# GpSimd makes the two bf16 parts of the negated row maxima, and its turn runs in another order

## What is computed

```
ada = silu(c) @ W_ada + b_ada                      # six modulation vectors
h = layernorm(x) * (1 + scale_msa) + shift_msa
q, k, v = split(h @ W_qkv + b_qkv)                 # 16 heads of 9 channels
attn = softmax(q * 9**-0.5 @ k.T)                  # over 256 tokens
x = x + gate_msa * (attn @ v @ W_proj + b_proj)
h = layernorm(x) * (1 + scale_mlp) + shift_mlp
x = x + gate_mlp * (gelu(h @ W_fc1 + b_fc1) @ W_fc2 + b_fc2)
U = qr(P).Q;  A = skew(silu(c) @ W.T + b);  R = expm(A)
out = x + ((x @ U) @ R - x @ U) @ U.T              # a rotation in 64 dimensions
```

## Time and profile before

| | us |
|---|---|
| three timed runs | 388.78, 390.67, 393.87 |
| their median | 390.67 |
| the profiled execution | 386.43 |
| its span, first to last instruction | 384.6 |

### The profile page before, as it was taken

One profiled execution on the slowest core, in us unless ns is written; L12 is line 12 of the kernel. 1 busy time (PEld: TensorE's weight loads), 2 busy tenths in 40 slices (PEclk: granted clock), 3 DMA queues, 4 the chain that ended last, 5 costly groups with the idle time before them and its releaser, 6 DMA issues.

```text
span 384.6 us, 7566 instructions
## 1 busy us (share of the span) xinstructions
PE 315.6 (82%) x2645; PEld 191.5 (50%) x2645; DVE 255.3 (66%) x791; ACT 144.6 (38%) x262; POOL 113.1 (29%) x271
## 2 busy tenths in 40 slices
PE   2888866986987889797889798989759999996687
PEld 1333423543444445454546455556546666664556
DVE  6856668578768877879888888864433554555433
ACT  2111113576674553545554555554202223321010
POOL 5813505006019046026053152020261333300000
PEclk9999998699998885899998998999957999999855
DMA  3922311114511212201212100000000000000003
GB/s 116 282 69 84 93 51 46 49 56 104 158 30 45 84 41 53 71 18 49 79 46 62 36 3 3 2 3 2 3 0 0 2 0 1 2 0 2 0 1 123
DMA packets 20202, 17.95 MB, mean 47 GB/s; under 512 B 3524, under 2 KB 18005, under 8 KB 20040
## 3 DMA queue, kind: packets, MB, share of 16 engines
q1 hardware_dynamic: 19556, 16.34, 15.6%
q10 hardware_dynamic: 610, 1.14, 1.0%
HBM read 12.28 MB, written 4.81 MB: 44 GB/s over the span
## 4 chain that ended last, share of the span: by engine, by line
PE 57%; DVE 27%; issue 7%; POOL 4%; ACT 3%; DMA 0%; DVEq 0%; POOLq 0%; ACTq 0%
DVE nm L912 11%; PE pst L264 10%; PE m L642 5%; PE m L483 5%; PE ps L449 5%; PE pst L265 5%; DVE gp L722 3%; PE m L286 3%; PE pst L470 3%; PE m L270 3%; PE pst L381 3%; DVE gm L723 2%; PE m L264 2%; PE pst L490 2%; DVE nmb L922 2%
## 5 line engine op out<-in xcount | busy, mean ns | idle before, releaser
L912 DVE TENSOR_REDUCE nm<-ps 128x2 f32<-128x512 f32 x128 | 87.7, 689 | 32.3 <-PE ps L449 29.2
L1144 ACT ACTIVATE pex<-pst 128x1024 f32<-128x1024 f32 x64 | 65.6, 1025 | 28.5 <-PE pst L470 27.8
L449 PE MATMUL ps<-ks,qs 54*128 54x256 bf16 x256 | 29.5, 309 | 29.3 <-DVE nm L912 28.7
L751 DVE TENSOR_SCALAR pm<-m 64x1 f32<-64x1 f32 x64 | 13.6, 213 | 43.7 <-PE m L286 43.2
L1434 POOL TENSOR_TENSOR qkr<-qk,parts 96x768 f32<-96x768 f32 x6 | 9.8, 1636 | 103.7 <-ACT parts L1125 103.7
L483 PE MATMUL m<-pex,ve 128*32 128x256 f32 x512 | 37.7, 416 | 0.0
L1447 POOL TENSOR_TENSOR xin<-xin,res 128x288 f32<-128x288 f32 x16 | 12.8, 799 | 76.3 <-DVE res L941 76.3
L449 PEld LDWEIGHTS ps<-ks,qs 54*128 54x128 bf16 x256 | 11.4, 102 | 42.5 <-issue 37.2
L270 PE MATMUL m<-gm,ident 64*64 64x65 f32 x126 | 24.3, 282 | 7.0 <-DVE gm L723 3.9
L286 PE MATMUL m<-qst,ident 64*64 64x64 f32 (+42 forms) x128 | 19.9, 235 | 11.1 <-DVE qst L757 11.1
L470 PE MATMUL pst<-qs,ks 56*128 56x256 bf16 x256 | 27.6, 295 | 1.0 <-ACT pex L1144 0.7
(11 more groups left out here) (246 smaller groups left out, 584.4 us busy)
## 6 DMA issues: line engine op xcount, KB each, us to landing
scr_qk<-parts SPq DMA_DIRECT2D x24, 144.0 KB, 2.0
qs<-scr_qk SPq DMA_DIRECT2D x96, 36.0 KB
ks<-scr_qk SPq DMA_DIRECT2D x72, 36.0 KB
gates<-scr_ada SPq DMA_DIRECT2D x2, 576.0 KB, 6.6
out_dram<-xin SPq DMA_DIRECT2D x8, 144.0 KB, 1.9
wr<-in_L_cond_W_dram SPq DMA_DIRECT2D x1, 1134.0 KB
xin<-in_x_dram SPq DMA_DIRECT2D x1, 864.0 KB, 5.4
ks<-scr_qk ACTq DMA_DIRECT2D x24, 36.0 KB
```

The source lines that it names most:

```text
L449: ins = mm(ps[e][:, L * i:L * i + L], qs[64 * e:64 * e + KS, b % 3, 2 * g + i, 128 * lt:128 * lt + 128], ks[64 * e:64 * e + KS, b % 3, 2 * ...
L912: nc.vector.tensor_reduce(nm[:, lt, e, 2 * g:2 * g + 2], ps[e][:, :].rearrange("p (h l) -> p h l", h=2), AX.X, ALU.max, negate=True).then_ ...
L1144: nc.scalar.activation(pex[:, n % 4, :, :], pst[0][:, :, :], ACT.Exp, scale=ATT_SCALE).then_inc(s("exp_done"), 1)
```

## The change

VectorE keeps `shift` for batch 0 only, in turn -1. For batches 1 to 7 GpSimd makes the same two instructions. VectorE now waits, before the first reductions of each half, until GpSimd has read the `nm` of the batch before. GpSimd's turn becomes: `shift(t, 1)`, `normalise(t + 3)`, `added`, `shift(t + 1, 0)`, `basis_norms`, `mlp_deviations`, `weight_parts`, `split`, and the mask.

```diff
@@ def maximum(b, n, e):   (VectorE)
                 dve.wait_ge(s(f"max{e}_filled"), NS * b + n + 1)
+                if b and n % (NS // 2) == 0:
+                    dve.wait_ge(s("shift_ready"), 2 * (b - 1) + n // (NS // 2) + 1)
@@ def turn_a(t):   (VectorE)
                     if n == 3:
-                        if real(t + 1):
-                            shift(t + 1, 0)
+                        if t == -1:
+                            shift(0, 0)
                         if t == EXPM:
                             polynomial()
...
-                    if n == 7 and real(t + 1):
-                        shift(t + 1, 1)
+                    if n == 7 and t == -1:
+                        shift(0, 1)
@@ (GpSimd)
+            def shift(b, hf):
+
+                for e in range(2):
+                    pool.wait_ge(s(f"max{e}_done"), NS * b + 4 * hf + 4)
+                await_fill(pool, f"nmT{hf}", b - 1)
+                heads = nm[:, :, :, 4 * hf:4 * hf + 4]
+                then(nc.gpsimd.tensor_copy(nmb[:, :, hf, :, 0, :], heads))
+                nc.gpsimd.tensor_tensor(nmb[:, :, hf, :, 1, :], heads, nmb[:, :, hf, :, 0, :], ALU.subtract).then_inc(s("shift_ready"), 1)
...
             for t in range(-1, B):
+                if t > 0:
+                    shift(t, 1)
+                if t >= 0 and t + 3 < B + 2:
+                    normalise(t + 3)
                 if real(t - 2):
                     added("proj", t - 2, res[:, :, :], "x1_ready")
+                if t >= 0 and real(t + 1):
+                    shift(t + 1, 0)
                 if t == BASIS_TURN:
                     basis_norms()
+                if real(t - 2):
+                    mlp_deviations(t - 2)
                 if t == 2:
                     weight_parts(1, wfc1_b, "mlp_loaded", 96, slice(3 * C, 3 * C + FF))
                 if real(t + 3):
                     split(t + 3)
-                if real(t - 2):
-                    mlp_deviations(t - 2)
-                if t + 4 < B + 2:
-                    normalise(t + 4)
                 if t == 2:
                     pool.wait_ge(s("up_loaded"), 16 * (R // 2))
```

## The result

| us | before | changed |
|---|---|---|
| median of four timed runs of each | 389.73 (388.26 to 393.87) | 378.17 (377.82 to 379.81) |
| the profiled execution | 386.43 | 378.52 |
| its span | 384.6 | 376.4 |

The ratio is 0.9711 [0.966, 0.9763]. The two profiled executions differ by 7.9 us (forecast 7.4), the two medians by 11.6.

The account below looks back on a forecast made before the run. Turn ends were taken as bound by VectorE, and VectorE by GpSimd. 4.0 + 0.3 + 1.6 + 1.5 = 7.4 us off 386.43 gave 379.0 profiled, ratio 0.981, 383.2 us timed; range 378.5 to 389.5.

Parts of the forecast that it names:

- turn 2 into turn 3: Gain of 0.3 us, bounds -0.7 to +1.3; `weight_parts` could hold line 722 in slot 6 by up to 1.2.
- slot 3 of turns 3 to 6: Cast and remainder leave VectorE's part of the chain there: 0.4 us for each of four turns, 1.6 us.
- the stall only moves: Rival: line 722 in slot 0 waits on behind `split`; only 2.8 us gained, 387.8 us timed; chance 0.22.
- the first term: Ends of turns 0, 1, 3 and 4: the next reduction no longer waits for the held cast, 1.0 us each, 4.0 us.
- GpSimd's pair: Two 128x16 instructions per half on GpSimd, 0.25 us each plus 0.1 gap, 0.6 us; in time for line 458.
- The rival of the dear pair: Pair takes 4 us, TensorE waits at line 458 in turns 1 to 5: 3.4 us slower, 394.1 timed; chance 0.06.
- the whole order: GpSimd's rearranged turn, with `normalise` behind `shift(t, 1)` and `mlp_deviations` ahead of `split`: no effect on time.
- VectorE's new wait: Slots 0 and 4: VectorE waits for a `shift` made a turn or half a turn before; costs nothing.
- No DMA moves: No DMA changes place except those that follow `split`; counted as nothing.
- The clock: Four TensorE clock dips after ends of turns 0, 1, 2 and 4 may shrink: 0 to 4.6 us, 1.5 taken.
- the carrying over from the profiled execution to the timed median: Timed median lies 1.1% above the profiled execution; ratio 0.981 applied to 390.67 gives 383.2 us.
- the clock comes back whole: Rival: all four dips' VectorE idle time is regained, 5.9 + 4.6 = 10.5 us, 380.0 us timed; chance 0.20.

Follow-up runs that it names:

- the relief alone: Kernel before, GpSimd unchanged, VectorE making the second half's cast and remainder one reduction later, in slot 0 of the next turn: 386.46 us, ratio 0.9888.
- the cut `split`: Changed kernel with `weight_parts` early and most `up` row DMAs later in turn 2, and `split`'s first and third instructions each made as three: 373.28 us, ratio 0.9585.
- the old order: Kernel before with the pair moved to GpSimd, whose other calls keep their order, so the second half's pair stands behind `normalise`: 399.32 us, ratio 1.0207.
- the second trace: Profile from the repeat of the changed kernel, nothing altered: 377.06 us, ratio 0.9745 against the kernel before.
- the second trace of before: Profile from the kernel before run unchanged against itself: 389.72 against 390.38 us, ratio 1.002; the profile itself took 389.1.
- the order alone: Kernel before with GpSimd's turn in the new order, VectorE keeping cast and remainder: 386.28 us, ratio 0.9776; repeated with more runs, 388.68 us, ratio 0.9933.
- the two edits of turn 2: Changed kernel with `weight_parts` ahead of `shift(3, 0)` and 20 of 24 `up` row DMAs behind it on SyncE: 378.7 us, ratio 0.9668.
- The kernel with the fewest stalls: Changed kernel with `weight_parts` early, most `up` row DMAs later, and `split`'s first and third instructions each made as three: 373.28 us, ratio 0.9585.

## Why the prediction came out as it did

**The stalls: right, and by the mechanism given.** The ends of turns 0, 1, 3 and 4 gave 1.2 + 1.0 + 0.9 + 0.9, that is 3.9 before rounding (forecast 4.0), turn 2 into turn 3 gave 0.4 (0.3), slot 3 of turns 3 to 6 gave 1.7 (1.6). Line 722 was reached as `split` ended, as worked out, and wasn't held in slot 0, so "the stall only moves" fell for this change. It holds one step further on, where slot 7 is made quicker. The kernel with the relief alone shows the first term on the clock of the timed runs: 0.9888.

The rule of the Trainium skill ("SBUF — State Buffer", "Who interferes with whom"), that the shared port pair is held for the whole instruction and the other side blocks, agrees with the cut `split`: the longest line 722 went from 1.51 us to 0.62 as the instruction beside it went from 1.63 to 2.15 / 3 = 0.72. That whoever issues first decides isn't borne out by the starts in the profile, which need not be the moments of issue: line 722 at 131.86 began 0.04 us ahead of GpSimd's line 1383 and was held to its end, whereas at 115.70 it began 0.06 us behind GpSimd's cast and took its usual 0.21.

**GpSimd's pair: right.** 0.20 + 0.24 us where 0.25 each was taken. Line 458 never waited for it. The rival of the dear pair was priced on the wrong quantity: 3 us of queueing in front of the pair would have done the same, as the old order shows (1.0207). The prediction said that `normalise` goes behind it, but put the whole order at "nothing"; the order is what keeps the change from being slower.

**VectorE's new wait: right.** The profile names GpSimd as releaser of three reductions, 0.2 us each, of which this is one:

```profile
179.60 0.69 DVE L914 TENSOR_REDUCE nm<-ps 128x2 f32<-128x512 f32 x1 [0.21 <-POOL nmb L1453]
```

The value that it asks for was reached half a turn earlier, and in the kernel before about the same gap follows line 880 in that slot (185.04 + 0.68 to 185.87). It is a name that fell in the gap, not a wait.

**Turn 2: half right.** The hold in slot 6 was foreseen at "up to 1.2". It came (1.32 us), but in this trace it cost nothing, since TensorE at 0.64 was the later one; at full clock it costs 0.6, and in the second trace it didn't occur. The relief of slot 7 that was set against it did not come, and "No DMA moves" overlooked that TensorE, being earlier, would meet SyncE's queue: 1.05 us of waiting, worth about 0.2. What either costs doesn't show in the time.

**The step that failed: "The clock ... I take a third, 1.5 us", and with it the carrying over from the profiled execution to the timed median by 1.1%.** On the pair of profiled executions the sum held term by term. The turn ends gave 3.9 + 0.4 and slot 3 gave 1.7, that is 6.0 where 5.9 was forecast. The other 3.3 of the 9.3 us up to (7, 7) lie in slots with a dip on one side or the other, the -1.6 of turn 2 among them; 1.1 was lost again behind the turns. So what isn't stalls is 2.2 on this pair, against the 1.5 taken for the clock, inside its bounds of 0 to 4.6. On the medians it was worth more, some 4 us by the estimate above, and there the miss arose. The prediction took the 1.1% between the profiled execution of before and its median as a factor that the changed kernel would have too. It had not: the changed kernel's profiled execution lies at its median (378.52 against 378.17), that of before 3.3 us under its own (386.43 against 389.73). In the turns the second trace of before has 34 us at the lower level, the first 30, the changed kernel 19, and the second traces of the two kernels are 12.4 us apart at (7, 7), not 9.3.

What was measured by itself adds up to about the whole: relief 1.1%, slot 3 0.4% from the rows, some 4 us or 1.1% that go with the clock by estimate, 2.6% of the 2.6 to 2.9. The relief alone left the clock where it was, and the clock of the order alone can't be told from that of before (67 and 72 us at the lower level against 83 and 76, each pair on one chip, with a spread as wide). Why the changed kernel has less lower clock isn't shown.

The rival "the clock comes back whole" named 380.0 for the timed median and was nearest. The case for giving it more weight was in the times shown: with three runs from 388.78 to 393.87 and a profile at 386.43, the profiled execution lay under all the timed ones, so what the change could win back in a usual one could be more than in that one trace.

## What to carry to other kernels

Where a small VectorE instruction ends exactly as a long GpSimd one does, price the long one, and cut it short if GpSimd has time: cutting two into thirds, with the two edits of turn 2, took the ratio here from 0.971 to 0.959. When work is moved to another engine, its place in that queue counts for more than its duration; 0.45 us of work cost 16.6 us of waits in the wrong place. When a slot gets longer and a held instruction stands in it, read TensorE's idle time and clock in that slot before the hold gets the blame: here 1.6 us beside a hold of 1.3 were the clock's. And before a dip of the clock is priced from one trace, compare that execution with the timed ones: if it lies under all of them, the usual execution has more to win.

## What was not expected of the hardware

One kernel, unchanged, took 383.07 to 394.78 us over all its executions here, and two of its traces, equal to 0.4 us up to (3, 0), stood 3.0 us apart one way at (4, 4) and 3.0 the other way at the end of the turns, by where the granted clock fell. The kernel with the fewest stalls had only some 6 us of its turns at the lower level; more matmuls brought less time at the lower level in the kernel before, in an idle slot and in a busy one, and no gain.

A hold can outlast the instruction that it began with. In the first trace of the order alone, line 722 was held through the rest of one GpSimd instruction and all of the next, 1.96 us, though it had begun 0.32 us ahead of the second:

```profile
138.84 1.27 POOL L1385 TENSOR_TENSOR wpart<-wrest,wpart 17x576 bf16<-17x576 f32 x1
139.76 1.96 DVE L722 SCALAR_TENSOR_TENSOR gp<-gm,gp,below 64x1 f32<-64x1 f32 x1
140.08 1.63 POOL L1434 TENSOR_TENSOR qkr<-qk,parts 96x768 f32<-96x768 f32 x1
```

A GpSimd power of 128x2 at 175.20, 0.73 us long, did not hold a line 722 at 175.56 (0.21 us) in the kernel before, whereas the subtractions of `split` did each time that they met.
